# Router logits of the first eight token tiles as 16-bit halves in three passes

## What is computed

```python
x = x + _L1_gnn_ref(_layernorm(x), edge_index, W, b)      # the tile "x4" of the kernel
xt = _layernorm(x)                                        # 1250 x 512
logits = xt @ Wr + br                                     # Wr is 512 x 8
probs = softmax(logits); G = max(probs); idx = argmax(probs)
y = G * (relu(xt @ W1[idx] + b1[idx]) @ W2[idx] + b2[idx])
```

## Time and profile before

| | |
|---|---|
| median of three runs | 529.25 us (528.96 to 532.93) |
| profiled execution | 533.77 us, of it 532.0 us span from the first to the last instruction |
| TensorE busy | 486.3 us, 91% of the span |
| VectorE busy | 429.0 us, 81% |
| ScalarE busy | 335.7 us, 63% |
| mean granted TensorE clock | 0.986 of full speed |
| the stage of the change | about 373 to 435 us of the span |

### The profile page before, as it was taken

How to read it: one execution, slowest core, us unless ns; L and a number is a source line. 1 busy time by engine, 2 the same in 40 slices (tenths; PEclk the granted TensorE clock), 3 DMA queues, 4 the chain that set the end, 5 groups by cost and what they waited for, 6 DMA issues and landing times.

```text
span 532.0 us, 11423 instructions
## 1 busy us (share of the span) xinstructions
PE 486.3 (91%) x4369; PEld 361.9 (68%) x4370; DVE 429.0 (81%) x874; ACT 335.7 (63%) x636; POOL 81.9 (15%) x94
## 2 busy tenths in 40 slices
PE   3999999993899999999998999989899999999994
PEld 3877776761899998997887644444466697776662
DVE  7958889896999999876888778975877787986961
ACT  7356666668799999972775723435444558866820
POOL 5000000000000000001221201213244411222232
PEclk9999999997899999999999899999999999999999
DMA  7970000002011111001000293000011129975111
GB/s 200 311 275 1 1 2 1 2 1 103 2 51 55 56 72 71 2 10 72 2 1 1 99 329 146 1 0 4 1 42 42 62 66 380 338 236 182 55 57 55
DMA packets 25267, 45.10 MB, mean 85 GB/s; under 512 B 6977, under 2 KB 7013, under 8 KB 25212
## 3 DMA queue, kind: packets, MB, share of 16 engines
q1 hardware_dynamic: 23228, 39.16, 21.5%
q0 software_dynamic: 1952, 5.18, 2.6%
q10 hardware_dynamic: 32, 0.01, 0.0%
HBM read 33.23 MB, written 11.95 MB: 85 GB/s over the span
## 4 chain that ended last, share of the span: by engine, by line
PE 36%; DVE 20%; DMA 5%; issue 5%; POOL 4%; ACT 3%; POOLq 0%; DVEq 0%
PE sums L1690 13%; PE sums L1526 7%; PE sums L1703 5%; PE sums L1915 4%; DMA out<-aux 2%; DMA aux<-xperm_scratch 2%; DVE st L901 2%; POOL row L528 2%; PE sums L1886 2%; DVE work L1156 1%; PE sums L1504 1%; DVE big L1319 1%; POOL out L512 1%; PE sums L1680 1%; ACT rings L570 1%
## 5 line engine op out<-in xcount | busy, mean ns | idle before, releaser
L1690 PE MATMUL sums<-big,work 128*128 128x130 f16 x1080 | 66.4, 223 | 8.7 <-DVE work L1156 8.7
L1690 PEld LDWEIGHTS sums<-big,work 128*128 128x128 f16 x1080 | 63.7, 100 | 10.2 <-issue 6.2
L1591 PE MATMUL sums<-big 128*128 128x180 f16 x320 | 60.2, 272 | 1.0 <-DVE big L1005 1.0
L1005 DVE TENSOR_TENSOR big<-mid 128x1024 f16<-128x1024 f16 (+1 forms) x88 | 59.4, 732 | 0.0
L1791 PE MATMUL sums<-mid 128*128 128x512 f16 x200 | 47.2, 379 | 0.0
L1703 PE MATMUL sums<-big,mid 128*128 128x260 f16 x400 | 47.0, 275 | 0.1
L1550 PE MATMUL sums<-big,rings 128*128 128x512 f16 x120 | 45.2, 377 | 0.4
L595 ACT ACTIVATE mid<-sums 128x180 f32 x80 | 26.5, 332 | 28.6 <-PE sums L1598 27.7
L1703 PEld LDWEIGHTS sums<-big,mid 128*128 128x128 f16 x400 | 38.2, 96 | 7.5 <-issue 0.3
L683 ACT ACTIVATE aux<-aux,small 128x1250 f16<-128x1250 f32 x32 | 40.9, 1326 | 2.5 <-DVE work L1156 1.7
L683 ACT ACTIVATE mid<-aux,small 128x1250 f16<-128x1250 f32 x32 | 40.8, 1323 | 2.4 <-DVE work L1156 2.4
(11 more groups left out here) (322 smaller groups left out, 1098.8 us busy)
## 6 DMA issues: line engine op xcount, KB each, us to landing
big<-in_L_ffn_W SPq DMA_DIRECT2D x10, 1024.0 KB, 9.7
mid<-in_L_ffn_W SPq DMA_DIRECT2D x6, 1024.0 KB, 14.1
xperm_scratch<-work SPq DMA_DIRECT2D x1, 5753.0 KB, 18.7
aux<-thr_scratch SPq DMA_DIRECT2D x8, 640.0 KB, 3.8
aux<-xperm_scratch SPq DMA_DIRECT2D x8, 523.0 KB, 3.9
row<-in_x SPq DMA_DIRECT2D x1, 1280.0 KB
aux<-in_L_gnn_Ws SPq DMA_DIRECT2D x4, 256.0 KB, 4.6
row<-in_x SPq DMA_DIRECT2D x1, 1024.0 KB, 7.9
```

What stands on the lines that cost most here:

```text
L1005: return V.tensor_tensor(out.rearrange("p c (v two) -> p c v two", two=2), values.rearrange("p (v two) -> p v two", two=2).unsqueeze(1).to ...
L1591: mm(count_bank(base, k)[:, 0:RW], L_ring[:, slot, k * CH + j, :], R_ring[:, slot, k * CH + j, :], start=j == 0, stop=False)
L1690: ins = mm(acc_region(h, t), weighted[i // 2 % NC][:, s % 2, t * P:(t + 1) * P], VP[:, s, part, h, :, :].rearrange("p b f -> p (b f)"), st ...
```

## The change

For the tiles 0 to 7 (`SPLIT_T = 8`) the router's logits are made from 16-bit halves. ScalarE's copy out of PSUM writes the high half (`xTs`, which lies in the same memory as `xT_ring`) and signals `xT_hi` rather than `xT_ready`. VectorE makes the low half with `xT_low` (line 924), which signals `xT_ready`; the call stands in VectorE's loop behind the wait for `x4_made` of tile t and ahead of the statistics of tile t, and treats tile t - 1. `Wr` times 256 is cut into halves once, by two VectorE instructions ahead of the loop. TensorE runs `linear16` (12 matmuls) in place of `linear`. The scale 1/256 of these logits is put into a column `rs_ws`, one more small VectorE instruction per tile. Tiles 8 and 9 stay as they are.

```diff
+SPLIT_T = 8
+        wr16, at = carve(small, at, [2, K, E1], F16)
+        rs_ws, at = carve(small, at, [T])
             def rows_copy(t):
                 if t >= 2:
                     a.wait_ge(sem("linD"), t - 1)
-                ln_copy(3 * T + t, bank[t % 2], xT_ring[:, t % 2, :, :], "xT_ready")
+                if t < SPLIT_T:
+                    ln_copy(3 * T + t, bank[t % 2], xTs[:, t % 2, 0, :, :])
+                else:
+                    ln_copy(3 * T + t, bank[t % 2], xT_ring[:, t % 2, :, :], "xT_ready")
             def logits(t):
-                V.scalar_tensor_tensor(lg[:, t, :], bank[2 + t % 2][:, 0:E1], row[:, t, D + 1:D + 2], offs[:, t, :], ALU.mult, ALU.add).then_inc(sem("lg_made"), 1)
+                scale = rs_ws[:, t:t + 1] if t < SPLIT_T else row[:, t, D + 1:D + 2]
+                V.scalar_tensor_tensor(lg[:, t, :], bank[2 + t % 2][:, 0:E1], scale, offs[:, t, :], ALU.mult, ALU.add).then_inc(sem("lg_made"), 1)
             def row_offsets(t):
+                if t < SPLIT_T:
+                    V.tensor_scalar(rs_ws[:, t:t + 1], row[:, t, D + 1:D + 2], 1.0 / WS, None, ALU.mult)
+            link(V.tensor_scalar(wr16[:, 0, :, :], Wr[:, :, :], WS, None, ALU.mult))
+            V.scalar_tensor_tensor(wr16[:, 1, :, :], Wr[:, :, :], WS, wr16[:, 0, :, :], ALU.mult, ALU.subtract)
             for t in range(T - 1):
                 v.wait_ge(sem("x4_made"), t + 1)
+                if t >= 1:
+                    xT_low(3 * T + t - 1, bank[(t - 1) % 2], xTs[:, (t - 1) % 2, :, :, :])
                 ln_stats(3 * T + t, x[:, t, :], row[:, t, D:D + 2])
                 if t >= 1:
                     logits(t - 1)
             def lin_d(t):
-                linear(xT_ring[:, t % 2, :, :], lambda k: Wr[:, k, :], bank[2 + t % 2][:, 0:E1], "linD")
+                if t < SPLIT_T:
+                    linear16(xTs[:, t % 2, :, :, :], wr16, bank[2 + t % 2][:, 0:E1], "linD")
+                else:
+                    linear(xT_ring[:, t % 2, :, :], lambda k: Wr[:, k, :], bank[2 + t % 2][:, 0:E1], "linD")
```

## The result

| | before | after |
|---|---|---|
| median | 531.13 us (8 runs, 528.34 to 533.89) | 535.87 us (8 runs, 534.49 to 537.79) |
| profiled execution, and its span | 533.77 us, 532.0 | 535.66 us, 533.5 |
| `relu` of tile 0 to `relu` of tile 9 | 51.99 us | 57.91 us |

The ratio is 1.0091, 95% interval [1.0057, 1.0125]: slower by 0.9%. The three runs of before known at the prediction had a lower median, 529.25.

The account below looks back on a forecast made before the run. The loop agg, relu, GpSimd's add, VectorE's statistics, logits, one-hot, ranks sets the pace, TensorE 0.2 us behind. Seven tiles at 0.71 (5.0 us) plus 1.0 for the first give 6.0: 529.25 becomes 535.2 us, range 533.3 to 539.5.

Parts of the forecast that it names:

- The low half lies in the loop: VectorE, between the wait for `x4_made` and the statistics: `xT_low` delays the statistics by 0.60 us per tile.
- TensorE's wait: TensorE ahead of the passes: `lin_d` waits for the low half, leaving TensorE idle 1.10 us per tile.
- The passes: TensorE, router logits: twelve 16-bit passes at 57 ns a pair take 0.68 us, for 0.91 us of eight float32 ones.
- late logits: VectorE's logits, waiting for TensorE's result at about 4.1 to 4.2 against 4.16: 0.03 us added per tile.
- The scale column: VectorE behind the one-hot row: `rs_ws` delays `token_low` and so GpSimd's add and `x4_made` by 0.07 us per tile.
- The step: Time from one `relu` to the next, tiles 1 to 7: 0.71 us longer each, 5.0 us in all.
- The first tile: Tile 0, with the halves of `Wr` (about 0.42 us) and `xT_low` (0.60): `ranks` later, +1.05 us.
- The clock rival: TensorE's pauses halve its clock; `agg` matmuls would add 4.4 us a tile, total over 560 us; chance 0.02.
- Dear passes: Rival on TensorE's passes: a 16-bit pair costs 114 ns like float32, tile +1.33 us, total 540.2 us; chance 0.10.
- GpSimd goes first: Rival: GpSimd's add starts ahead of `token_low` as a rule; a tile takes 6.53 us, total 534.1 us; chance 0.25.
- The add pushed back further: Rival: `place` falls wholly before GpSimd's add, which waits some 0.3 us more a tile; total 537.3 us; chance 0.08.
- The cover: Rival: TensorE bounds the stage, low half covered; eight tiles save 0.23 us each, total 527.4 us; chance 0.05.

Follow-up runs that it names:

- e1: Kernel before, plus one VectorE instruction per tile of the low half's kind and size at its place, writing scratch; float32 passes kept: ratio 1.0075.
- e3: Changed kernel with `xT_low` moved ahead of the wait for `x4_made`, nothing left out: ratio 1.0003.
- e9: Changed kernel with the twelve passes of each of the eight tiles made twice over: one execution, 536.56 us.
- e10: Changed kernel without the scale column `rs_ws`, `Wr` cut into halves unscaled: one execution, 538.40 us.
- e4: Changed kernel with twelve dummy matmuls of zeros in TensorE's pause ahead of the first tile's passes: ratio 1.0106.
- e2: Changed kernel without the low half of x; twelve 16-bit passes kept, using the high half instead, so logits less exact: ratio 1.0020.
- e11: Changed kernel with the low half ahead of the wait for `x4_made`, no scale column, and the cut of `Wr` ahead of `split_w` of expert 0: ratio 1.0006.
- e5: The changed kernel itself measured again against the kernel before, in a later comparison: ratio 1.0126.
- e7: Changed kernel with the low half ahead of the wait for `x4_made` and `token_low` right behind the logits: ratio 1.0054.
- e6: Kernel before with `token_low` of a tile moved from behind `place` to right behind the logits, nothing else: ratio 0.9967.

## Why the prediction was right, and where its terms were off

The forecast was 535.2 us from a median of 529.25, that is +6.0 or 1.1%; measured are +4.7 (0.9%), and 1.3% in the second comparison. The stage shows +5.92 for a sum of 6.0. Two things in this are luck. The time came within 0.7 us of the forecast because the median of before, from more runs, rose by 1.9 us while the difference was 1.3 smaller than forecast. And the stage's sum is close because errors cancel: the first two steps grew by 1.95 (1.05 predicted), the third by 0.07 (0.71 predicted), the last six by 3.9 (4.3 predicted). The ratio of the first comparison also lies just inside 1%, to which I had given 0.35, and that of the second just outside.

*The low half lies in the loop.* Right: predicted start at 2.54 and 0.60 for what follows, measured 2.42 and 0.61 in the tile shown. e1 has its loss alone, e3 takes it away by order in all steps but the third.

*TensorE's wait.* Its length was about right (1.10 predicted, 1.11 to 1.31 in the last six of these tiles), its harmlessness only half seen: the forecast had TensorE tie with VectorE at `ranks`, 5.58 against 5.57. It doesn't tie.

*The passes* are the mis-sized term. I took 57 ns a pair, from loads with 130 columns behind them; measured are (0.37 - 0.10) / 11 = 25 ns, the passes took 0.29 to 0.32 us and not 0.68. So the 57 ns of the earlier trace rows can't be the load's, which is the same here: they go with the 130 columns. The measured 25 lies just above my lower bound of 20, for which I had no row. It changed nothing, since VectorE set the step (e9); so the 0.03 for late logits was not due either. In the Trainium skill, page "TensorE: Matmul & The Clock Gate", the table of "Back-to-back issue gap" gives matmuls of 1 to 64 columns, without their loads, about 60 cycles or 25 ns. The trace has the same 25 ns for pairs with loads; the two figures that I had set against Rows 7 (107 ns a load, 81 ns a pair) are both far above it.

*The scale column.* Right in size and in way: 0.07 predicted, 0.04 to 0.08 in e10.

*The step.* +0.71 a tile predicted, +0.65 in the last six. The third step hardly grew (5.92 to 5.99). With TensorE at half clock ahead of it, VectorE ended `token_low` at 380.44, as the next add began (380.35), and the add took 1.09:

```profile
379.75 0.69 DVE L1380 TENSOR_TENSOR aux<-rings,aux 128x512 f16<-128x512 f32 x1
...
380.35 1.09 POOL L531 TENSOR_TENSOR row<-row,work 128x512 f32<-128x512 f32 x1 [5.80 <-ACT work L779]
```

That is 0.6 us under the forecast, and it goes with the low clock: at a clock of 1.00 (e4) this step is 6.48, +0.56.

*The first tile.* +1.05 predicted; the second step grew by 1.66 and the first by 0.29, together 1.95. The halves of `Wr` cost 0.33 (371.15 to 371.48, 0.42 predicted). The 2.60 us pause stood in the sum: it had the first load of the passes at 378.77, and the loads of the ten matmuls ahead of them end at 376.06 in the timeline of before:

```profile
374.13 1.93 PEld L1791 LDWEIGHTS sums<-mid 128*128 128x128 f16 x10
```

But I asked what the pauses of 1.1 us do to the clock and never what this one does. The clock rival, to which I gave 0.02, came in this tile alone. Without it (e4) the first two steps grew by 0.95, near the sum's 1.05; net of the third step the clock is worth 0.58 us.

*The other rivals.* Dear passes: refuted by 25 ns. GpSimd goes first, as a rule: no, the add took 1.62 to 1.83 us from the fourth step on. The add pushed back further: no, it starts behind `token_low` as in the kernel before. The cover: it needed another order, and even with it (e3) the time is that of before. One slip stands in the range: half of the 4 us above 537.3 is 539.3, not 539.5.

## What to carry to other kernels

An instruction put behind a wait is not in the idle time in front of that wait: if the wait heads the loop that sets the pace, the instruction costs its full spacing in nearly every turn, though the engine is busy only 73% of it. Before work is moved from the busiest engine to another, follow the loop once round; here TensorE was busy 6.00 of 6.00 us, and making its work 0.6 us shorter in every tile gave nothing (e2, e11). And look at the first turn by itself: here its pause was the longest, and the clock fell behind it.

## What of the hardware I had not expected

A pair of a 16-bit 128x128 load and an 8-column matmul takes 25 ns, against 114 ns for one of the two pairs of a float32 block, so twelve passes cost a third of eight. A pause of 2.6 us in a stage at full clock was followed by about 3 us near 0.50, in all four traces that have it (the change, e5, e9, e10); a pause of 1.93 us at the same place (e3, e7) left the clock at 1.00, and so did pauses of 1.1 to 1.3 us in six later tiles. GpSimd's add and some of VectorE's instructions stop each other both ways: the add took 1.5 to 1.8 us behind `token_low` and 1.1 to 1.3 without it (e6), and `sel` took 0.7 to 1.4 instead of 0.33 us behind the add (e6), while the low half, with one operand in PSUM, ran through the add in e3 without either growing.
